# Feed-forward and first cross attention of batches 1 to 3 interleaved with the heads of attention

## What is computed

```python
x = x + tanh(g_xattn[0]) * L0_xattn(layernorm(x), ctx)   # kv = ctx@W_k.T + b_k; out = p@kv; sim = out@kv.T/16
                                                         # layernorm(sim)*gamma + beta, then softmax over 256
x = x + tanh(g_ffn[0]) * L0_ffn(layernorm(x))            # rows to 8 bits, weights ternary:
                                                         # bit_linear(silu(bit_linear(x)) * bit_linear(x)), 1024 hidden
x = x + tanh(g_xattn[1]) * L1_xattn(layernorm(x), ctx)   # 16 heads, rotary queries of 192, latent keys of 64
x = x + tanh(g_ffn[1]) * L1_ffn(layernorm(x))            # 8 experts, top 2, capacity 320, 1024 hidden
```

## Time and profile before

| | us |
|---|---|
| median of 3 runs | 611.46 (610.19 to 612.35) |
| the profiled execution, its own time | 612.25 |
| span of its profile | 610.4 |

### The profile page before, as it was taken

How to read it: one execution, slowest core, us unless ns; L and a number is a source line. 1 busy time by engine, 2 the same in 40 slices (tenths; PEclk the granted TensorE clock), 3 DMA queues, 4 the chain that set the end, 5 groups by cost and what they waited for, 6 DMA issues and landing times.

```text
span 610.4 us, 11625 instructions
## 1 busy us (share of the span) xinstructions
PE 458.7 (75%) x4466; PEld 346.7 (57%) x4466; DVE 431.1 (71%) x960; ACT 262.3 (43%) x588; POOL 236.2 (39%) x240
## 2 busy tenths in 40 slices
PE   1884626766367799899879997799741899999991
PEld 0564502434255577678657775677631477777781
DVE  3248985899855587788868977887733388878870
ACT  0444432544331545545525543455510365556630
POOL 1057760111103123333223421542032347777875
PEclk9996866878558899999969997999785699999997
DMA  7891092000051000000000410100001346676624
GB/s 209 276 338 21 6 362 103 0 2 0 1 184 58 2 1 2 2 2 2 1 25 14 124 51 2 37 20 2 5 31 38 84 162 182 183 183 183 161 23 44
DMA packets 37687, 47.69 MB, mean 78 GB/s; under 512 B 7424, under 2 KB 32768, under 8 KB 37440
## 3 DMA queue, kind: packets, MB, share of 16 engines
q1 hardware_dynamic: 29552, 40.97, 20.8%
q0 software_dynamic: 4224, 4.79, 5.0%
q10 hardware_dynamic: 3856, 1.18, 0.9%
HBM read 41.10 MB, written 8.55 MB: 81 GB/s over the span
## 4 chain that ended last, share of the span: by engine, by line
PE 48%; DVE 28%; ACT 6%; issue 5%; DMA 5%; POOL 5%; ACTq 3%; POOLq 0%; SPq 0%; DVEq 0%; another core or an unknown queue 0%
PE psum L1292 9%; PE psum L1501 7%; PE psum L1352 5%; PE psum L1514 4%; PE psum L1337 3%; PE psum L1319 3%; PE psum L1366 3%; PE psum L1312 3%; DMA se<-in_w 3%; PE psum L1392 3%; ACT lw L634 2%; DVE se L957 2%; ACT lw L607 2%; DVE am L855 2%; DVE lw L845 2%
## 5 line engine op out<-in xcount | busy, mean ns | idle before, releaser
L455 POOL TENSOR_TENSOR lw<-lw 128x512 f32<-128x512 f32 x48 | 60.7, 1269 | 135.6 <-DVE lw L913 135.4
L641 ACT ACTIVATE lw<-psum 128x512 f16<-128x512 f32 x64 | 38.2, 597 | 84.5 <-PE psum L1352 84.3
L1292 PE MATMUL psum<-lp 128*128 128x256 f16 x576 | 70.2, 277 | 5.5 <-DVE scat L1026 3.7
L634 ACT ACTIVATE lw<-psum,nmax 128x256 f32<-128x256 f32 x128 | 59.2, 471 | 11.7 <-DVE nmax L924 11.7
L1292 PEld LDWEIGHTS psum<-lp 128*128 128x128 f16 x576 | 54.8, 99 | 14.2 <-DVE scat L1026 3.9
L514 POOL TENSOR_TENSOR lw<-lw 128x320 f16<-128x320 f32 x64 | 47.9, 749 | 36.1 <-DVE lw L1099 32.7
L1501 PE MATMUL psum<-lw,se 128*128 128x320 f16 x384 | 56.6, 307 | 1.0 <-issue 0.7
L929 DVE TENSOR_TENSOR lw<-psum,lw 128x512 f16<-128x512 f32 x64 | 43.8, 684 | 15.7 <-ACT lw L641 14.6
L702 ACT ACTIVATE lw<-psum,b1w 128x320 f16<-128x320 f32 x64 | 33.7, 527 | 46.8 <-PE psum L1501 46.8
L1099 DVE TENSOR_SCALAR lw<-psum,b1w 128x320 f32<-128x320 f32 x64 | 35.3, 551 | 20.3 <-ACT lw L702 19.7
L1352 PE MATMUL psum<-identf,lw 128*128 128x128 f32 x256 | 43.7, 296 | 7.5 <-DVE lw L929 4.0
(11 more groups left out here) (201 smaller groups left out, 1022.1 us busy)
## 6 DMA issues: line engine op xcount, KB each, us to landing
se<-in_w SPq DMA_DIRECT2D x16, 1024.0 KB
dispatch<-in_empty SPq DMA_DIRECT2D x4, 662.5 KB, 9.6
lw<-dispatch SPq DMA_DIRECT2D x8, 265.0 KB
lp<-in_Wq SPq DMA_DIRECT2D x1, 2048.0 KB, 14.2
se<-in_WoT SPq DMA_DIRECT2D x1, 2048.0 KB, 16.6
lp<-in_w_kc_q SPq DMA_DIRECT2D x1, 1536.0 KB, 18.5
x_sb<-in_x SPq DMA_DIRECT2D x2, 512.0 KB, 6.0
se<-in_gate_wT SPq DMA_DIRECT2D x1, 1024.0 KB, 9.5
```

The lines of the kernel that those rows point to most:

```text
L455: nc.gpsimd.tensor_tensor(rope[:, c % QT, :], t1[:, c % 2, :], t2[:, c % 2, :], ALU.add)\
L634: A_(e_sb[:, n % 2, st * S:(st + 1) * S], bank[3 + n % 2][:, st * S:(st + 1) * S], ACT.Exp, bias=nmax[:, n % 2, st:st + 1], accum_out=esum ...
L1292: ins = M(tile_bank(c)[:, half * S:(half + 1) * S], m1[w][:, kc, half, col:col + P], (yth, ytl)[a][:, kc, b * S:(b + 1) * S], start=(n == ...
```

## The change

New constants say how much goes ahead of attention: NL0 = 2 batches of the first cross attention and NB0 = 1 batch (NT0 = 2 tiles) of the feed-forward. The rest stands in the loop over heads, which now begins at n = -9 (LEAD). `ffn_at(n, r)` gives batch b at head n = 16(b-1) + r, `xat_at` likewise: for batches 1 to 3 of the feed-forward r runs from -9 (statistics) to 8 (rows ready for the queries), for batches 2 and 3 of the first cross attention from -20 to -10.

A tile's feed-forward is also done otherwise there. ACT scales the products (`unquant`), POOL adds the bias over all 1024 columns (`add_bias`, two for each tile) and multiplies gate and value over all 1024 (`gate_value`); before, DVE did scale and bias in one instruction for each 512 columns, and 640 of the 1024 columns of the product. The silu of each tile stands between exponentials on ACT. The two `key_side` products for each step stand together in four steps, instead of one in each of eight. Query tiles use bank 0 of PSUM alone, and stand one each at the third and fourth head of a group and the first head of the next. `rotate_context` and the context's turning move to the start. The splitting of the first expert's weights (`split_high`, `split_low`) moves from heads 24 to 36 to heads 44 to 56. In routing, PE waits for v_cnt (the counts are read) where it waited for v_idx (the whole of `route_place`), and logits use bank 1.

```diff
+NB0 = 1
+NL0 = 2
+NT0 = TPB * NB0
+LEAD = 9
...
             g, h = n // G, n % G
-            return [c for c in {2: [QT * (g + 2)], 3: [QT * (g + 2) + 1, QT * (g + 2) + 2]}.get(h, []) if c < QT * NGB]
+            c = {2: QT * (g + 2), 3: QT * (g + 2) + 1, 0: QT * (g + 1) + 2}.get(h, -1)
+            return [c] if 0 <= c < QT * NGB else []
+
+        def ffn_at(n, r):
+
+            b = (n - r) // NH + 1
+            return [b] if (n - r) % NH == 0 and NB0 <= b < B else []
+
+        def xat_at(n, r):
+
+            b = (n - r) // NH + 1
+            return [b] if (n - r) % NH == 0 and NL0 <= b < B else []
...
-            return bank[(0, 1, 0)[c % QT]]
+            return bank[0]
...
@@ GpSimd @@
+            def add_bias(i, w):
+
+                pool.wait_ge(a_mgv, 4 * i + 2 * w + 2)
+                if i == 0 and w == 0:
+                    pool.wait_ge(d_gb, 48)
+                dst = (vm, gm)[w][:, i % 2, :]
+                nc.gpsimd.tensor_tensor(dst, dst, (vb_b, gb_b)[w], ALU.add).then_inc(g_mb, 1)
+
+            def gate_value(i):
+                pool.wait_ge(a_msilu, i + 1)
+                nc.gpsimd.tensor_tensor(vm[:, i % 2, :], vm[:, i % 2, :], gm[:, i % 2, :], ALU.mult).then_inc(g_mu, 1)
...
+                for b in xat_at(n, -20):
+                    std(0, b)
+                for b in xat_at(n, -13):
+                    scale_std(b)
+                for b in xat_at(n, -12):
+                    scale_shift(b, zm)
+                for b in ffn_at(n, -9):
+                    std(1, b)
+                for b in ffn_at(n, -5):
+                    add_bias(tile_a(b), 0)
+                for b in ffn_at(n, -4):
+                    add_bias(tile_a(b), 1)
+                for b in ffn_at(n, -2):
+                    gate_value(tile_a(b))
+                for b in ffn_at(n, -1):
+                    add_bias(tile_b(b), 0)
+                for b in ffn_at(n, 0):
+                    add_bias(tile_b(b), 1)
+                for b in ffn_at(n, 2):
+                    gate_value(tile_b(b))
+                for b in ffn_at(n, 6):
+                    std(2, b)
...
@@ ScalarE @@
-            for s in range(NT + 2):
-                for t in ([0, 1] if s == 0 else [s + 1] if s + 1 < NT else []):
+            for s in range(NT0 + 2):
...
+                for u in (2 * s, 2 * s + 1):
+                    key_side(u)
+                if 1 <= s <= NT0:
...
+            def unquant(i, w):
+
+                t = NT0 + i
+                if i >= 2:
+                    act.wait_ge(v_mhq, i - 1)
+                for u in range(2):
+                    act.wait_ge(p_mgv, 4 * i + 2 * w + u + 1)
+                    A_((vm, gm)[w][:, i % 2, 512 * u:512 * u + 512], bank[1 + u][:, :], ACT.Copy,
+                       scale=(svs, sgs)[w][:, t:t + 1]).then_inc(a_mgv, 1)
+
+            def silu(i):
+                act.wait_ge(g_mb, 2 * i + 2)
+                A_(gm[:, i % 2, :], gm[:, i % 2, :], ACT.Silu).then_inc(a_msilu, 1)
...
-                if n in (24, 28, 32, 36):
-                    split_high((n - 24) // 4)
+                if n in (44, 48, 52, 56):
+                    split_high((n - 44) // 4)
...
+                for b in ffn_at(n, -6):
+                    q_turned(b)
+                for b in ffn_at(n, -5):
+                    unquant(tile_a(b), 0)
+                for b in ffn_at(n, -4):
+                    unquant(tile_a(b), 1)
+                for b in ffn_at(n, -3):
+                    silu(tile_a(b))
+                for b in ffn_at(n, -1):
+                    unquant(tile_b(b), 0)
+                for b in ffn_at(n, 0):
+                    round_up(tile_a(b))
+                    unquant(tile_b(b), 1)
+                for b in ffn_at(n, 2):
+                    silu(tile_b(b))
+                    h_turned(tile_a(b), bank[2])
+                for b in ffn_at(n, 3):
+                    round_up(tile_b(b))
+                for b in ffn_at(n, 4):
+                    h_turned(tile_b(b), bank[1])
+                for b in ffn_at(n, 8):
+                    yth_of(b, bank[2])
...
@@ VectorE @@
+                for b in xat_at(n, -20):
+                    stats_of(b, v_st[0])
+                for b in xat_at(n, -19):
+                    rows_normed(0, b, v_y0)
+                for b in xat_at(n, -13):
+                    sim_stats(b, bank[2])
+                for b in xat_at(n, -12):
+                    sim_normed(b, bank[2], zm)
+                for b in xat_at(n, -11):
+                    sim_max(b, zm)
+                for b in xat_at(n, -10):
+                    sim_update(b, zm)
+                for b in ffn_at(n, -9):
+                    dve.wait_ge(v_u0, TPB * (b + 1))
+                    stats_of(b, v_st[1])
+                for b in ffn_at(n, -8):
+                    q_scales(b)
+                for b in ffn_at(n, -7):
+                    q_rows(b, qm, v_mq)
+                for b in ffn_at(n, -1):
+                    peak(tile_a(b))
+                for b in ffn_at(n, 1):
+                    h_rows(tile_a(b))
+                for b in ffn_at(n, 3):
+                    ffn_out(tile_a(b), bank[1][:, 0:D])
+                    peak(tile_b(b))
+                for b in ffn_at(n, 4):
+                    h_rows(tile_b(b))
+                for b in ffn_at(n, 6):
+                    ffn_out(tile_b(b), bank[2][:, 0:D])
+                    dve.wait_ge(v_u1, TPB * (b + 1))
+                    stats_of(b, v_st[2])
+                for b in ffn_at(n, 7):
+                    rows_normed(2, b, v_y2)
+                for b in ffn_at(n, 8):
+                    ytl_of(b, bank[2])
...
@@ TensorE @@
-            for g in range(2):
-                for c in range(QT * g, QT * g + QT):
-                    queries(c)
-                if g == 0:
-                    latent(0)
-            scores(0)
-            for n in range(NHB):
+            for n in range(-LEAD, NHB):
...
+                for b in ffn_at(n, -6):
+                    if latents >= 1:
+                        pe.wait_ge(v_qz, latents)
+                    turn_q2(b)
+                for b in ffn_at(n, -5):
+                    pe.wait_ge(a_mq, b - NB0 + 1)
+                    gate_or_value(tile_a(b), 0)
+                for b in ffn_at(n, -4):
+                    pe.wait_ge(a_mgv, 4 * tile_a(b) + 2)
+                    gate_or_value(tile_a(b), 1)
+                for b in ffn_at(n, -1):
+                    for bx in xat_at(n, -17):
+                        pe.wait_ge(a_yT0, bx + 1)
+                    gate_or_value(tile_b(b), 0)
+                for b in ffn_at(n, 0):
+                    pe.wait_ge(a_mgv, 4 * tile_b(b) + 2)
+                    gate_or_value(tile_b(b), 1)
+                for b in ffn_at(n, 3):
+                    ffn_product(tile_a(b), bank[1][:, 0:D])
+                for b in ffn_at(n, 4):
+                    pe.wait_ge(v_mfo, tile_a(b) + 1)
+                    turn_h(tile_b(b), bank[1])
+                for b in ffn_at(n, 6):
+                    pe.wait_ge(v_qz, latents)
+                    ffn_product(tile_b(b), bank[2][:, 0:D])
+                for b in ffn_at(n, 8):
+                    pe.wait_ge(v_mfo, tile_b(b) + 1)
+                    turn_y2(b, bank[2])
```

688 lines of the change are left out of this document (395 added, 293 removed).

## The result

The changed kernel takes 647.02 us (median of 4 runs, 644.18 to 648.93) against 611.87 for the kernel before: a ratio of 1.058, interval 1.053 to 1.063. It is slower by 35 us where 16 less were forecast, and outside the range of 572 to 626.

The account below looks back on a forecast made before the run. Feed-forward was taken as a chain filling no engine, heads as nearly bound by PE. From 612.25 us, 55 less in front, 27, 7.5 and 5 more in heads gave 596.8, median 596 us; range 572 to 626.

Parts of the forecast that it names:

- The front: Everything before the first exponential: 17 us earlier first product, 44 less feed-forward, 6 more after it; 55 us less (40 to 66).
- For each group of four heads I take the larger of DVE's sum ... and PE's: Heads: the larger sum of existing plus added work, with 1.2 us waiting for PE, sets each group; 27 us more.
- 12.5 on top: Heads: 7.5 us for silus and table loads on ACT at five heads, 5 us for DVE beside POOL.
- The second way to the 27 us: Heads: a routed batch put 9.4 us on DVE and cost 5.7; at that rate 46 us on DVE cost 28.
- Steps are two heads apart: Moved feed-forward steps in the heads: their spacing was the argument against chains between engines delaying the heads; no size given.
- the first rival: Heads 3, 6, 15 and the same of later batches: chains across engines delay maxima; 72 us more, 629 us, chance 0.20.
- The query tiles one by one cost nothing in the sum: Third tile before the latent keys: PE's 3 us of work covers DVE and POOL; if not, 0.5 us a group, 8 us.
- Batch 3's heads: Heads of groups 12 to 15: only routing and the moved splits there, 1 us less.
- free time takes all (576): Heads: the engines' free time takes nearly all added work, heads grow by 18 to 20 us; 576 us, chance 0.22.
- Exclusion of DVE by the work given to GpSimd: Heads 0 to 40: DVE's SBUF instructions and POOL's exclude each other, 32 us instead of 5; 623 us, chance 0.08.
- the front isn't freed: Front: transfers or folded weights hold the first product, 17 and 44 us become 5 and 35; 617 us, chance 0.05.
- Signs: Marks named beforehand in front and heads: event times, group lengths, PE's waits under 20 us, DVE over 85% busy, clock 0.85.

Follow-up runs that it names:

- The narrow runs: Changed kernel, moved steps of batches 2 and 3 on 32 columns, on DVE, on ScalarE, or on both and PE: 631.17, 632.43 and 619.46 us.
- The first run: Changed kernel with the second tile's rounding, rounded rows, copy and turning each one head later: 640.43 us, ratio 1.049.

## Why the prediction was wrong

**The front was right.** First product 78.3 (forecast 77), last update 115.3 (112), first exponential 144.9 (145), 54.7 us less (55). That it is right to the microsecond is luck: other profiles of the same front ended 3 to 7 us earlier.

**The added work was near.** In the heads PE is busy for 37.4 us more (28 forecast, at the full clock; part of it ran slower), DVE for 51.3 (46), ScalarE for 47.9 (17.5 for each of three batches, less what stands ahead), GpSimd for 56.1 (some 50).

**The step that failed** is "For each group of four heads I take the larger of DVE's sum ... and PE's". It says that an engine's free time takes added work until it is full. The narrow runs show that it doesn't: ScalarE, which had half of its time free, passed on half of each us. As I read the order, a head is a ring, from scores to maximum, exponentials, turning, copy and low half to context, with each link on another engine and only one or two heads under way at once. A step that stands between two links delays the ring even where its engine has time later. The predicted sum for this was 27 us and 12.5 on top; the moved work cost 75.4 (90.7 less 15.3). In groups 4 to 10 at least 40% of it was the length of the work; the rest, with what is left of that length, was not taken apart.

**The second way to the 27 us** failed in a reading that the trace of before could have corrected. It took a routed batch as 5.7 us over plain groups, by spreading 17.2 us over three batches. But batches 1 and 2 took 67.0 and 66.7 us, some 10 over the 56.8 of four plain groups. Batch 3, which is routed too, took 52.6 up to head 63, having no query tiles to make in its last two groups. So where 9.4 us on DVE came on top of full groups, with some waits of PE, they had cost 10 us and not 5.7. At that rate 46 us on DVE would have been 49 us, and the sum some 619. It also makes the forecast's base for batches 1 and 2 (62.5 us) too low by 4 us each.

**"Steps are two heads apart"**, the argument against the first rival, holds for neither tile. The first tile's gate product, maximum, rounding, rounded rows and turning stand one head apart, at heads -2 to 2. The second tile's maximum and rounding both stand at head 3, its rounded rows, turning and copy at head 4. The rows of the order were there to read. PE's 28.4 us at that turning are the sign. The first run shows that they are not the price, 3.5 to 4.5 us being all that came back.

**"The query tiles one by one cost nothing in the sum"** named the right risk, at 8 us. All edits of the heads' order together cost 15.3, without the gain at the counts more. The cover counted on, 3 us of PE's work, had to hold two engines' queues and not two instructions. The term was sized by the third tile alone and left out that each tile now waits for the one before it in bank 0.

**Batch 3's heads** were to take 1 us less, and took 12.5 more: 4.7 with the query tiles' order alone and 3.9 with the choice of experts and the dispatch at their new heads alone. The 3.9 left are about what the slower group 12 makes, which the same code does not always show.

**Rivals.** The first, chains inside the heads, is nearest in kind. At 72 us for the heads and 629 in all it is still short of 90.7. That free time takes all (576) is refuted. Exclusion of DVE by the work given to GpSimd is refuted as a main cost at 2 to 3 us, and that the front isn't freed by the trace.

**Signs.** Groups of over 22 us in heads 0 to 31 were named as the mark of an error and are there four times (22.3 to 31.0). Groups without added work were to stay at 14.2 us; groups 12 to 14 took 19.6, 18.3 and 18.2. DVE over 85% busy in heads 4 to 7 and 20 to 27 was the mark of the sum; it was 70%, 72% and 86%. PE's waits for exponentials in that stretch, 14.9 us, stayed under 20 as forecast (they are 24.4 over all heads), so this sign did not see the loss. The granted clock over heads 0 to 31, which was not to fall below 0.85, was 0.91 (144.87 to 324.18 us).

**What stays open.** The 29 us left in groups 4 to 10 were not taken apart into waits, the instructions' least length, table loads and GpSimd's work; taking away the largest wait only moved it. Nor was it tried whether the same steps, spread over more heads with banks of their own, would fit; the kernel uses all eight banks into which it divides PSUM in the heads as it is, and a place for the third tile without bank 0 was not tried.

## What to carry over

Before moving work into a pipelined loop, don't compare sums of busy time per engine: see how many iterations the loop keeps under way, and price each added instruction that stands between two links of the ring at a good part of its length, whichever engine it is on (in this loop 0.7 on DVE and 0.5 on ScalarE). Then compare that with what the same work costs where it is: here some 22 us for a batch of feed-forward in the heads against some 20 ahead of them (79.1 us for four), so the move had nothing to win in this form. Buffers that the moved steps take from the loop (here one PSUM bank, and with it the order of the query tiles) are part of the price, and are tested most cheaply by making that edit alone in the kernel before.

## What was not expected of the hardware

Ten table loads of 1283 ns cost 5 to 6 us in all between the exponentials. GpSimd's addition of 128x512 took 2.12 us beside one DVE instruction and 1.27 alone; a DVE split of 1.22 us took 3.33 beside two such additions, and a normalisation on DVE 1.36 us for 0.40. PE's granted clock was 0.83 over a group in which it waited 3.4 us at one place and over one in which it waited 11.0, where plain groups had 1.00. So a wait can have a second price in the products behind it (0.63 to 0.69 us for 0.38 to 0.43 at the latent keys). At the same place a wait of 2.3 us went with a clock of 1.00 and a group of 15.8 us instead of 19.6.
